# Attention stage of a three-layer block on one core: statistics of the last piece and normalisation of the last two tiles put at other places in two engines' queues

## What is computed

```python
def _L0_attn_ref(x, w_qkv, w_proj, b_proj):
    qkv = x @ w_qkv.T
    q, k, v = jnp.split(qkv, 3, axis=-1)
    q, k, v = relu(to_bhdn(q)), relu(to_bhdn(k)), to_bhdn(v)
    ksum = k.sum(axis=-1)
    z = 1.0 / (jnp.einsum('bhd,bhdn->bhn', ksum, q) + eps)
    context = jnp.einsum('bhdn,bhen->bhde', v, k)
    out = jnp.einsum('bhde,bhen->bhdn', context, q) * z[:, :, None, :]
    ...
    return out @ w_proj.T + b_proj

x = x + 0.5 * _L0_ffn_ref(_layernorm(x), ...)
x = x + _L0_attn_ref(_layernorm(x), ...)
x = x + 0.5 * _L0_ffn_ref(_layernorm(x), ...)
```

## Time and profile before

| what | us |
|---|---|
| median of 3 runs | 1249.27 |
| lowest and highest | 1247.13, 1252.63 |
| the profiled execution | 1243.24 |
| its span | 1241.5 |
| PE busy in the span | 1148.4 |
| DVE busy | 852.7 |
| ACT busy | 759.6 |
| POOL busy | 698.1 |

### The profile page before, as it was taken

How to read it: one execution, slowest core, us unless ns; L and a number is a source line. 1 busy time by engine, 2 the same in 40 slices (tenths; PEclk the granted TensorE clock), 3 DMA queues, 4 the chain that set the end, 5 groups by cost and what they waited for, 6 DMA issues and landing times.

```text
span 1241.5 us, 26349 instructions
## 1 busy us (share of the span) xinstructions
PE 1148.4 (93%) x6696; PEld 904.6 (73%) x6696; DVE 852.7 (69%) x2774; ACT 759.6 (61%) x1698; POOL 698.1 (56%) x850
## 2 busy tenths in 40 slices
PE   7988999999999967899998999889998999999995
PEld 5555555899999946777887878545557999999653
DVE  6788784566666655768878786677844666666488
ACT  4454441688888845675655653544415888888398
POOL 3577776488888854000411503356763888887810
PEclk9999999999999998999999999899999999999997
DMA  9922227556555523012320400114585555555398
GB/s 360 309 91 95 98 104 201 172 172 174 171 172 156 164 104 105 32 38 68 112 72 24 133 22 35 35 69 141 171 210 180 173 170 174 173 157 162 119 400 333
DMA packets 94215, 181.53 MB, mean 146 GB/s; under 512 B 17624, under 2 KB 60400, under 8 KB 92022
## 3 DMA queue, kind: packets, MB, share of 16 engines
q1 hardware_dynamic: 66630, 110.44, 29.2%
q0 software_dynamic: 26016, 67.55, 15.3%
q10 hardware_dynamic: 1424, 1.86, 0.5%
HBM read 97.63 MB, written 86.08 MB: 148 GB/s over the span
## 4 chain that ended last, share of the span: by engine, by line
PE 58%; DVE 17%; ACT 11%; issue 5%; POOL 5%; DMA 3%; SPq 1%; DVEq 0%; ACTq 0%; POOLq 0%
PE bank L700 20%; PE bank L710 10%; PE bank L559 7%; PE bank L691 5%; POOL expert_rows L1683 4%; PE bank L575 4%; PE bank L806 3%; ACT rows L1021 3%; ACT w L1021 3%; DVE stat L1161 2%; PE bank L756 2%; PE bank L732 2%; ACT xn L1039 1%; PE bank L521 1%; ACT rows L898 1%
## 5 line engine op out<-in xcount | busy, mean ns | idle before, releaser
L700 PE MATMUL bank<-rows,att 128*128 128x128 f32 x2288 | 303.2, 276 | 0.3 <-ACT att L1010 0.3
L700 PEld LDWEIGHTS bank<-rows,att 128*128 128x128 f32 x2288 | 279.2, 192 | 0.8 <-ACT att L1010 0.6
L1683 POOL DMA_INDIRECT expert_rows<-rows,slots x160 | 155.4, 971 | 80.0 <-issue 57.3
L1010 ACT COPY att<-w 128x512 f32 x286 | 177.0, 619 | 10.2 <-issue 4.2
L1740 POOL DMA_INDIRECT routed_rows<-silu,rdest x160 | 158.3, 989 | 35.0 <-issue 24.6
L1458 DVE SCALAR_TENSOR_TENSOR rows<-bank,tile_b,att 128x128 f32<-128x128 f32 x286 | 100.1, 350 | 112.9 <-ACT att L1015 102.0
L710 PE MATMUL bank<-w,rows 128*128 x572 | 171.5, 382 | 4.3 <-DVE rows L1458 4.2
L1740 POOL DMA_INDIRECT routed_rows<-rows,rdest x126 | 124.7, 990 | 68.4 <-DVE rdest L1441 40.7
L1009 ACT COPY rows<-bank 128x256 f32<-128x256 f32 x286 | 106.6, 373 | 89.1 <-PE bank L691 86.9
L575 PE MATMUL bank<-ws,be 128*128 128x256 f32 x512 | 124.0, 388 | 8.6 <-DVE be L1364 8.6
L925 ACT ACTIVATE silu<-bank,bs 128x512 f32<-128x512 f32 x64 | 43.9, 686 | 127.6 <-PE bank L559 117.5
(11 more groups left out here) (212 smaller groups left out, 2156.9 us busy)
## 6 DMA issues: line engine op xcount, KB each, us to landing
rows<-expert_rows SPq DMA_DIRECT2D x286, 129.5 KB
rows<-routed_rows SPq DMA_DIRECT2D x32, 512.0 KB, 4.2
w<-routed_rows SPq DMA_DIRECT2D x10, 1024.0 KB, 10.9
out<-xres SPq DMA_DIRECT2D x16, 512.0 KB, 9.3
xres<-in_x SPq DMA_DIRECT2D x7, 1024.0 KB, 9.5
rows<-routed_rows SPq DMA_DIRECT2D x6, 1024.0 KB, 7.7
expert_rows<-pad SPq DMA_DIRECT2D x47, 129.5 KB, 14.0
w<-in_w SPq DMA_DIRECT2D x1, 4096.0 KB, 24.4
```

What stands on the lines that cost most here:

```text
L700: last = nc.tensor.matmul(rh_ps[t % RB][:, n * P:(n + 1) * P], m.rw13[:, t % RB, c * C + n * INTER:c * C + (n + 1) * INTER], m.rT[:, t % R ...
L1010: nc.scalar.copy(m.rw13[:, a % RB, :].rearrange("p (c n) -> p c n", c=KC), w13[:, :, bass.ds(expert_at(i + 2), C)]).then_inc(s.rw13_copied, 1)
L1683: nc.gpsimd.indirect_dma_start(out=d.xg, out_offset=bass.IndirectOffsetOnAxis(ap=m.slots[:, slots_of(r), k, i:i + 1], axis=0), in_=m.xs[bu ...
```

## The change

Two edits. On DVE `combine` of the last piece no longer takes its statistics; the new `measure_sums` does so, and it stands with `aggregate` behind `sum_keys(b, 1)`. On ACT the normalisation of tiles 6 and 7 stands behind the copy of the second transposed query bank (`copy_qT(b, 1)`) instead of ahead of the mixer's copy.

```diff
@@ -1124,11 +1124,12 @@
                 relu_q(b, 2)
                 following(range(4, 6))
                 relu_q(b, 3)
-                following(range(6, 8))
                 act.wait_ge(s.mixer_ready, b + 1)
                 nc.scalar.copy(m.m_sb.rearrange("p c n -> p (c n)"), g_ps[:]).then_inc(s.mixer_copied, 1)
                 for p in range(PAIRS):
                     copy_qT(b, p)
+                    if p == 1:
+                        following(range(6, 8))
                     if more:
                         a_copy_xT(b + 1, p)
                     else:
@@ -1471,7 +1472,7 @@
-            def combine(b, h):
+            def combine(b, h, measure=True):
                 n = PAIRS * b + h
                 y = m.ylq[:, n % YSLOTS]
                 dve.wait_ge(s.bias_added, BIASED.index(b) + 1)
@@ -1479,7 +1480,11 @@
                 dve.wait_ge(s.weighted, n + 1)
                 ch.then(TT(x, x, y[:, 0, :], ALU.add))
                 TT(x, x, y[:, 1, :], ALU.add).then_inc(s.combined, 1)
-                dve.wait_ge(s.combined, n + 1)
+                if measure:
+                    measure_sums(b, h)
+
+            def measure_sums(b, h):
+                dve.wait_ge(s.combined, PAIRS * b + h + 1)
                 stats(b, range(2 * h, 2 * h + 2))
@@ -1605,12 +1610,14 @@
                     steps(work, 1)
                 if more:
                     combine(b + 1, 2)
-                    combine(b + 1, 3)
-                    aggregate(s.a_stats_ready)
+                    combine(b + 1, 3, measure=False)
                 else:
                     negate_mean(BATCHES + EARLY)
                     route_stats(BATCHES + EARLY + 1)
                 sum_keys(b, 1)
+                if more:
+                    measure_sums(b + 1, 3)
+                    aggregate(s.a_stats_ready)
                 scale(b, 0)
                 if more:
                     a_negate_mean(b + 1)
```

## The result

| | median us | lowest to highest | ratio to before, 95% interval |
|---|---|---|---|
| before | 1248.28 (4 runs) | 1247.13 to 1252.63 | |
| after | 1237.21 (4 runs) | 1236.05 to 1239.21 | 0.9908 [0.9888, 0.9927] |

A forecast was written before the change was run, and what follows sets the result against it. PE's recurring waits in the attention stage, for DVE's key sums and ACT's copy, were taken as the bound; 5.0 + 5.6 = 10.6 us off the 1249.27 us median gave 1238.7 us, range 1233.5 to 1246.

The forecast's parts named there:

- Term A: DVE's key sums ahead of the statistics: PE's wait at L764 (spreading key sums) shrinks in even batches, 5.0 us.
- Term B: ACT's tiles 6 and 7 normalised behind the copies: PE's wait at output matmuls L806 shrinks in all batches, 5.6 us.
- The pair's room: ACT's two normalisations fit the gap ahead of the next batch's second transposed bank, with 0.8 us to spare.
- The root's cover: POOL's later reciprocal root ends 0.7 us before DVE's L1488 needs it; beyond that, each microsecond is paid four times.
- POOL's slack in batch 7: POOL's next root waits 4.25 us for DVE; later scatters and the batch's gain take 2.8 us, costing nothing.
- That the pair costs PE's next wait: Rival: ACT's two normalisations hold the second transposed bank, so the 5.6 us are given back; 1244.3 us, 10%.
- That the root runs only behind the scaling: Rival: POOL's root waits out DVE's scaling, L1488 1.85 us late in four batches; gain 3.2 us, 1246.1 us, 8%.
- That something else sets the batch's pace: Rival: something outside the two engines, such as arriving routed pieces, sets the pace; waits only move, 1249.3 us, 5%.
- That PE loses its clock: Rival: PE falls to half clock in the attention stage; two spells, 30 us, cost 15 and give 1253.7 us, 5%.
- the rule that the prediction weighed: Trainium skill: a two-SBUF-input DVE instruction and an SBUF-reading GpSimd one exclude each other, the later fully blocked; gain then 3.2 us.
- The prediction's row: Batch 2: DVE's L1497 starts inside POOL's root and takes 0.43 us, against 0.42 with POOL idle; no stop of DVE.

The follow-up runs named there:

- root taken twice: Both edits, with POOL taking each attention batch's reciprocal root twice, first into an unread tile; 1239.31 us, ratio 0.9956 to the kernel before.
- the pair alone: Kernel before with only ACT's normalisation of tiles 6 and 7 moved, DVE's order unchanged; 1238.32 us, ratio 0.9948.

## Why the prediction was right

**Term A**, 5.0 us: the spread's wait ended in batches 2, 4 and 6 for 1.67 us each where the forecast had 1.54, and the odd batches gave nothing, as said; 5.2 us from spread 0 on, and 0.43 ahead of it (forecast 0.4).

**Term B**, 5.6 us: 0.99 to 1.00 in the even batches (forecast 0.99), 0.37 to 0.39 in the odd ones (0.38), 0.63 in batch 7 (0.5); 5.7 us. The step that carried it, that in the odd batches the mixer itself sets the first copy, is right: ACT's mixer copy waits there for PE, here in batch 1:

```profile
546.30 0.59 ACT L1128 COPY rows<-bank 128x512 f32<-128x512 f32 x1 [0.49 <-PE bank L780]
```

The terms that the prediction names there, 545.08 + 0.47 + 0.59, come to 546.14 and not to its 546.24, which would be 0.48 us a batch. The 0.1 us that it adds without saying so is there: from the mixer's end to L806 the profile after has 1.16 us (546.27 to 547.43), where the named terms have 1.06.

**The covers** held where they were put. The pair's room was forecast at 0.8 us and is 0.78. The root's cover was forecast at 0.7 and is 0.59, mostly because the root took 2.00 us in place of 1.89. The prediction has four batches pay once the cover is gone; the root taken twice shows three, since in batch 0 the root ends at 498.08 (496.43 + 1.65) and its reader starts at 500.16. POOL's slack in batch 7 was forecast to fall from 4.25 to 1.45 and fell to 1.05.

**The rivals.** That the pair costs PE's next wait: no wait of that kind, and with the pair alone 5.7 us. That the root runs only behind the scaling: refuted by its rows, though it is held for a part of one instruction (last section). That something else sets the batch's pace: the distances fell by 1.0 to 2.05 us each. That PE loses its clock: the stage, 475.5 to 783.6 us after, has a granted clock of 0.99, with the half clock at its beginning only, where before (first row) had it too:

```profile
473.71:792.24 318.53, 299.91 (x1617) 251.36 (x1617) 238.58 (x636) 186.28 (x422) 77.81 (x80) 0.99 0.19 62
475.50:783.60 308.10, 299.70 (x1617) 252.21 (x1617) 237.79 (x636) 186.85 (x422) 74.95 (x78) 0.99 0.20 63
```

PE's busy time is the same, 300 us, now in 308 instead of 318.5 us.

**What the sum did not hold.** By the rows both edits are worth 11.4 us (10.3 from spread to spread, 0.63 behind batch 7's, 0.43 ahead of batch 0's), and 10.6 were forecast. The timed gains were 11.1, 13.6, 12.8 and 12.1 us, with intervals that hold 11.4, so it is partly luck that the first of them came so close to the forecast. Why the later ones lie 0.7 to 2.2 us above the rows is open.

The second layer behind the stage took between 439.8 and 444.1 us in the profiles, and two profiles of the same kernel differ there by 3.4 us. Most of that goes with PE's granted clock. In the four profiles of both edits the stretch from the gate to the end takes 450.7, 446.9, 450.3 and 447.8 us. An estimate of what it lost to the clock, in windows of 1 us the length times what the granted clock lacks to 1.00, gives 14.9, 11.7, 15.0 and 13.2 us; without that they agree within 1.2 us, at 434.6 to 435.8. Before has 449.3 us and 13.5 by the same estimate, so the 1.4 us by which the first profile after is longer there is clock as well. Why the stage begins at 473.7 to 477.1 us, behind a first layer at the full clock, is open. So a single profile's time tells less than the distances inside it, and the two profiled executions alone differ by 7.2 us.

## What to carry to other kernels

An instruction that nobody is waiting for can stand ahead of one that an engine is idle for, simply because the code reads better so: look at each recurring wait for what its releaser did just before, and ask whether that could stand behind. In this kernel such a move was worth about the smaller of the wait and the work moved, and only where the wait set the pace; it must be paid for at its new place: name the gap it goes into and check every instance of that gap, since one batch in eight may have something else in it. Where several waits repeat in a loop, count the distances between the same instruction in successive rounds; they repeat to a few hundredths of a microsecond where whole runs scatter by several.

## What the hardware showed beside that

POOL's roots of 128x8 elements take 1.63 to 1.67 us in most of their places and 1.89 to 2.08 us in the others. In the rows of eight profiles a root is longer where it starts while DVE has an instruction with two SBUF inputs under way, and by more the more of it is left: with 0.38 to 0.40 us left it takes 1.89 to 1.92, with 0.50 to 0.53 it takes 2.00 to 2.04, with 0.58 it takes 2.08. That is how it stands in batch 2 after: the scaling's L1516 runs from 575.51 to 576.20, the root starts at 575.70. Where the DVE instruction starts behind the root's start, the root keeps its length and the instruction its 0.69 us, as with root taken twice in batch 1:

```profile
537.53 1.64 POOL L1689 TENSOR_TENSOR rstd<-ve,minus_half 128x8 f32<-128x8 f32 x1
```

```profile
537.89 0.69 DVE L1517 TENSOR_TENSOR att<-be,att 128x512 f32<-128x512 f32 x1 [2.17 <-ACT att L1118]
```

So one half of the rule that the prediction weighed fits these rows: the root, coming later, is held by the DVE instruction that runs. The prediction's row could not show that, since it looked at DVE's side alone; the root's own 1.89 us there, against 1.67 in batch 7, was the sign. The other half does not fit: no DVE instruction is held for the root's span. The one row where DVE pays, and the root keeps its 1.63, has 0.80 us in place of 0.69, for an L1517 that starts 0.05 us ahead of a root (root taken twice, 693.83). In batches 2, 4 and 6 after the change the hold takes some 0.35 us (2.00 against 1.65) out of the root's cover, and it costs no time.
